# Order of the four single-precision matmuls that make the third channel tile

## The reference

```
x = x + L0(group_norm(x))   # 1x1 conv, depthwise 3/5/7, 1x1 conv, channel attention, 1x1 projection
x = x + L1(group_norm(x))   # 1x1 conv to q, k, v; channel attention; its result is one 192x192 matrix per image times the input
x = x + L2(group_norm(x))   # projection to x_in, delta, B, C; selective scan over 4096 positions; projection
x = x + L3(group_norm(x))   # 7x7 depthwise conv, mirrored borders
```

## Time and profile before

| | |
|---|---|
| median of 3 runs | 3204.47 us (3198.21 to 3208.03) |
| profiled execution, its time | 3192.12 us |
| profiled execution, its span | 3190.3 us |
| granted TensorE clock, mean | 0.862 |
| TensorE busy | 2387.6 us (75%) |
| VectorE busy | 1220.4 us (38%) |
| ScalarE busy | 978.0 us (31%) |
| GpSimd busy | 812.5 us (25%) |

### The profile page before, as it was taken

The page is one execution under the profiler, slowest core; times in us unless marked ns, Lnnn a source line. Parts: engine busy times, 40 slices in busy tenths (PEclk is TensorE's granted clock), DMA queues, the critical chain, the costliest instruction groups (busy, mean ns, idle before and its releaser), DMA issues. The chain is left out here.

```text
span 3190.3 us, 37429 instructions
## 1 busy us (share of the span) xinstructions
PE 2387.6 (75%) x15968; PEld 1379.6 (43%) x15968; DVE 1220.4 (38%) x1081; ACT 978.0 (31%) x1264; POOL 812.5 (25%) x321
## 2 busy tenths in 40 slices
PE   3877878739999999995697938678677877877022
PEld 1566666627777777772352112223132212321022
DVE  4333434310000000004402160799499728974722
ACT  2344444410000000002210011666367526650400
POOL 1433334300000000000000000578188607870310
PEclk9989989869999999997795565799899989998556
DMA  5899999962122112102000110000000000002389
GB/s 180 273 296 310 292 302 283 267 225 86 49 90 90 65 70 90 45 1 84 9 1 29 46 48 20 0 0 0 0 1 0 0 0 1 0 16 66 107 226 272
DMA packets 175035, 314.40 MB, mean 99 GB/s; under 512 B 7049, under 2 KB 130185, under 8 KB 166217
## 3 DMA queue, kind: packets, MB, share of 16 engines
q1 hardware_dynamic: 162216, 305.94, 31.4%
q10 hardware_dynamic: 12672, 6.29, 0.7%
HBM read 185.59 MB, written 125.04 MB: 97 GB/s over the span
## 5 line engine op out<-in xcount | busy, mean ns | idle before, releaser
L589 PE MATMUL ps<-mem 128*128 128x288 f16 x5376 | 677.0, 286 | 50.9 <-DMA mem<-depthwise_out 50.9
L589 PEld LDWEIGHTS ps<-mem 128*128 128x128 f16 x5376 | 519.3, 98 | 194.5 <-issue 66.5
L1350 POOL TENSOR_TENSOR mem<-mem 128x1024 f32<-128x1024 f32 x48 | 113.1, 2356 | 1632.9 <-ACT mem L1340 1632.9
L1353 POOL TENSOR_TENSOR mem<-mem 128x1024 f32<-128x1024 f32 x192 | 448.3, 2353 | 40.8 <-ACT mem L1324 40.5
L434 PE MATMUL ps<-mem 56*96 56x256 f16 x5184 | 325.7, 288 | 105.8 <-DVE mem L527 96.4
L1298 PE MATMUL ps<-mem 128*128 128x512 f32 x768 | 379.3, 617 | 16.1 <-POOL mem L1353 13.2
L434 PEld LDWEIGHTS ps<-mem 56*96 56x96 f16 x5184 | 312.0, 130 | 127.4 <-DVE mem L527 102.8
L1381 DVE TENSOR_TENSOR_SCAN mem<-mem,ps 128x1024 f32<-128x1024 f32 x144 | 337.9, 2347 | 60.7 <-ACT mem L1331 37.2
L804 DVE MEMSET mem<- 96x96 f32 x2 | 0.3, 138 | 860.9 <-DMA mem<-in_tri 860.9
L527 DVE TENSOR_TENSOR mem<-ps,mem 96x1024 f16<-96x1024 f32 x144 | 171.3, 1217 | 274.6 <-ACT mem L472 274.6
L503 POOL TENSOR_TENSOR mem<-mem 120x2304 f16<-120x2304 f32 x36 | 163.7, 4548 | 342.0 <-ACT mem L465 342.0
(11 more groups left out here) (179 smaller groups left out, 2392.2 us busy)
## 6 DMA issues: line engine op xcount, KB each, us to landing
depthwise_out<-mem SPq DMA_DIRECT2D x36, 1536.0 KB, 15.6
mem<-depthwise_out SPq DMA_DIRECT2D x16, 3328.0 KB, 10.9
mem<-in_wd SPq DMA_DIRECT2D x40, 1080.0 KB, 17.4
mem<-base_phases SPq DMA_DIRECT2D x72, 504.0 KB
base_phases<-mem SPq DMA_DIRECT2D x56, 576.0 KB, 10.5
mem<-l_planes SPq DMA_DIRECT2D x48, 252.0 KB
mem<-in_x SPq DMA_DIRECT2D x4, 2048.0 KB, 10.9
l_planes<-mem SPq DMA_DIRECT2D x2, 4032.0 KB, 13.3
```

Source lines behind the costliest of these rows:

```text
L589: ins = nc.tensor.matmul(ps[:, 2 * (i % 2) + h, 0:HALF], d, pw[0:rows, wa, k, HALF * h:HALF * h + HALF], start=(k == 0 and n == 0), stop=( ...
L1353: nc.gpsimd.tensor_tensor(hh[:, n % 4, :], hh[:, n % 4, :], cs[:, n % 2, :], ALU.mult).then_inc(hc_pool, 1)
```

## The change

In the two places that make output tile 2 the loop over the two images is split in two. Before, the order was: 128-row matmul of image 0, 64-row matmul of image 0, 128-row matmul of image 1, 64-row matmul of image 1. After, it is: 128-row matmul of image 0, 128-row matmul of image 1, 64-row matmul of image 0, 64-row matmul of image 1. The operands, the number of instructions, the accumulation and the semaphore update on the last one are the same.

```
@@ -103,6 +103,8 @@
     for b in range(B):
         lo = 64 * b
         nc.tensor.matmul(out[lo:lo + 64], wa[:, o0 + 128:o0 + 192], src[:, b, n0:n0 + n], start=True, stop=False)
+    for b in range(B):
+        lo = 64 * b
         last = nc.tensor.matmul(out[lo:lo + 64], wc[lo:lo + 64, o0 + 128:o0 + 192], src[lo:lo + 64, 2, n0:n0 + n],
                                 start=False, stop=True)
     return last
```

## The result

The changed kernel takes 3112.49 us (median of 4 runs, 3110.65 to 3116.22), the kernel before beside it 3206.25 us (median of 4, 3198.21 to 3219.32): ratio 0.9705, 95% interval 0.9671 to 0.974, 94 us less. The forecast was 45 us less with a lower end of 3136 us; the direction was right, the size too small by half and the range missed.

A forecast was written before the change was run, and what follows sets the result against it. No engine bounds the whole chain of blocks, but TensorE bounds tile 2's stretches. Shape changes 9.9, overlap 34.2 and group norms 1 us sum to 45 us: 3204.5 - 45 = 3159 us, range 3136 to 3196 us.

The forecast's parts named there:

- Where the time is: Tile 2's three stretches: TensorE ends last, so time taken from it comes off the span; readers, loads and stores stay hidden.
- Part 1, shape changes: Tile 2 in layers 1 and 2: two shape changes fewer a call, 0.141 or 0.197 us each; 9.9 us saved.
- Part 2, overlap: Tile 2 in layers 1 and 2: neighbours on separate array parts overlap, six streaming slots a call instead of eight; 34.2 us.
- B1 stands behind A2 and can start with it: Pair's instruction halves, A image 0, B image 1: in-order starts let only A2 and B1 overlap, three slots for four.
- Full overlap: Rival, tile 2: a pair takes two slots; 79 us gained in all, 3125 us; chance 6%.
- the middle: Overlap estimate chosen for tile 2: three slots a pair, 34.2 us saved, between nothing and 68.5 us.
- The clock in layer 1: Rival: layer 1's clock rises, its eight calls going from 5.49 toward 2.86 us; up to 21 us more; chance 10%.
- Part 3: Elsewhere: group norms save 1 us, range 0 to 2.4; readers and loads of the old x stay hidden.
- One pair only: Rival, tile 2: only one of the 128-row and 64-row pairs overlaps; 28 us gained, 3176 us; chance 12%.
- No single-precision overlap: Rival, tile 2: only the shape changes are saved, 10 to 11 us; 3194 us; chance 16%.
- nothing gained: Rival, tile 2: stepping between column halves costs what a shape change does, and nothing overlaps; 3204 us; chance 6%.
- clock falling in layer 2: Rival: the granted clock drops to 0.50 in layer 2's two stretches; slower, 3222 us; chance 5%.

The follow-up runs named there:

- e3: Changed kernel, but in tile 2's 512-column calls image 1's two matmuls go on image 0's place, so nothing can overlap; one run, 3172.08 us.
- e6: Changed kernel with two tile 2 calls issued together in the residual blocks, images 0,1,0,1 in layer 1 and 0,0,1,1 in layer 2; one run, 3117.95 us.
- e4: Changed kernel with every 64-row matmul of layers 1 and 2, all three tiles, made 128-row with zero weights for the other image; 3021.5 us.
- e5: Changed kernel with every second 512-column call in layers 1 and 2, all three tiles, issuing its 64-row matmuls first; 3046.25 us.
- e7: e4 with tile 2 in the order of before, image 0 twice, then image 1 twice; 3017.09 us.

## Why the prediction missed

- **Where the time is.** Right. TensorE ended last in all three stretches, all that was taken from it came off the span, and the readers, the loads of the old x and the stores stayed hidden.
- **Part 1, shape changes.** Right in mechanism and price: 0.141 us, by `e3` to 0.1 us over 16 calls. At 1.2 GHz the first call of `e3` takes 7.20 us (1776.81 to 1784.01), where the price of 0.197 us gives 7.19. Together 9.9 us of the gain. The trace agrees here with the Trainium skill (TensorEngine Tiling (Array Packing), section Tiling Modes), which says that a change of mode drains the engine and another tile of the mode does not. Each change costs 0.141 us and nothing overlaps across it, and within a pair of one shape both matmuls start together.
- **Part 2, overlap: the step that failed.** "B1 stands behind A2 and can start with it", three slots for four. The starts of the trace after show both images' first halves within 10 ns, then both second halves; `e6` shows that whole matmuls pass as well. The term, `e3` less after, is 24 x 1.70 = 41 us in layer 2, where the forecast had 20.6, and in layer 1 at 1.2 GHz 8 x (7.20 - 3.81) = 27 us, where it had 13.6. "Full overlap" stood among the rivals with 6%. The argument against it, that neighbours of one shape start in order, rested on rows in which every matmul used the same part of the array and so had to; those in the earlier trace rows, on different parts, were issued in turn and never put one in another's way. No row told the middle from the far end, and the two should have had chances nearer to each other.
- **The clock in layer 1: left out of the sum, and as a rival taken only with three slots.** Eight calls like the first (3.81 us) would be 30.4 us; they took 18.0, so 12.4 us come from the clock. The prediction gave this 10% and said that "the new order lies between these", which was the right reading: in `e3`, `e4` and `e5` the clock goes up with fewer shape changes. The mistake of the range was to treat full overlap and the rising clock as apart from one another, each as a case with the other left as forecast; with both, 45 + 34 + 12 is 91 us.
- **Part 3.** Group norms 2.4 us, the far end of the range, since both pairs overlap there too.
- **The other rivals.** One pair only: false; the 64-row pair, with different rows and columns but one PSUM bank, takes the same 1.01 us as the 128-row pair. The Trainium skill (TensorEngine Tiling (Array Packing), Restrictions and Gotchas) says that different row tiles cannot access one PSUM bank at the same time; this pair does, with columns that differ too. The Trainium skill (TensorE: Matmul & The Clock Gate, Part 3) says that weight loads overlap matmuls in flight only when the row group differs; the 128-row pair contradicts it, whose two matmuls have the same rows, start within 10 ns of each other and take 1.01 us together. No single-precision overlap, nothing gained, clock falling in layer 2 (it stayed at 1.00): all false.

The terms again, from the stretches: layer 1 42.8 us (forecast 16.8), layer 2 47.7 us (27.4), group norms 2.4 us (1).

## What to carry to other kernels

Before counting streaming time, look at the shapes of neighbouring matmuls: compare the distance of starts with that of a stream in one shape. Put matmuls of one shape and different column or row halves next to each other, and where a small one breaks the shape, widen it with zero weights: here the kernel whose products in layers 1 and 2 have one shape each takes 3021.5 us, 0.944 of before, and it needs no reordering (`e7`). When a cost has both an order and a clock in it, give the case in which both move at once a chance of its own.

## What the runs showed of the hardware

- A change of matmul shape cost 0.14 us at 2.4 GHz and 0.20 us at 1.2 GHz for 64 columns, and nothing overlapped across it (1.00 us a step before, whether or not the neighbour used other rows and columns). In one shape the next weights load under the running matmul (0.43 us from start to start for 512 columns in single precision); behind a change the first load starts with its own matmul.
- Single-precision matmuls on separate column halves run fully side by side: 1.01 us for two with 128 rows, 1.00 us for one, at 2.4 GHz and with the shape change behind them.
- A waiting matmul does not block later ones for other parts of the array: 0, 0, 1, 1 takes 3.74 us, as 0, 1, 0, 1.
- A TensorE that is busy without a gap can stay at 1.2 GHz when the shape changes at every matmul: 64.1 us of tiles 0 and 1 and 60.8 us of tile 2 one after the other in layer 1 before. The same products of tiles 0 and 1 in one shape reached 2.4 GHz and took 30 us. With the new order the clock rose 4 us into tile 2 of layer 1 (12 us in `e3`). A stretch with the same shape changes that began at 2.4 GHz stayed there for its 64 us (layer 2). By which measure the chip decides was not settled here.
